# Six-stage transformer kernel: new order for the first two cell blocks, maxima through TensorE, ffn weight preparation inside the scan stage

## The reference, cut to what matters

```python
x = x + _L0_xattn_ref(_layernorm(x), ctx_1024, ctx_1024, mask, ...)   # masked cross attention, 16 heads
x = x + _L0_attn_ref(_layernorm(x), context, Wq, Wk, Wv, Wout, bout)  # wide attention, 8 heads of 128, over 2 x 512 context rows
x = x + _L0_ffn_ref(_layernorm(x), ew, act_w, We, be, Wq, ...)        # cell: 6 nodes, each an attention over earlier nodes, edge weights We
x = x + _L1_xattn_ref(_layernorm(x), ctx_1024)                        # plain attention on the context
x = x + _L1_attn_ref(_layernorm(x), A, W_b, ..., W_o, b_o)            # scan: h[t] = a[t] h[t-1] + u[t], 16 states per sequence
x = x + _L1_ffn_ref(_layernorm(x), W_fc, ..., B_proj)                 # ffn 256 -> 1024 -> 256

# in the ffn, for W_fc and W_proj alike:
scale = jnp.max(jnp.abs(w)) / 127
wq = jnp.clip(jnp.round(w / scale), -128, 127) * scale
Wq = w + (wq - w)
y = x @ Wq.T + b + 2.0 * ((x @ A.T) @ B.T)                            # rank 16
```

## Time and profile before

| | |
|---|---|
| median of 3 runs | 3278.88 us (3271.15 to 3282.62) |
| the profiled execution | 3276.0 us, span 3274.2 us, mean TensorE clock 0.963 of full |
| PE busy | 3023.0 us (92%) |
| DVE / ACT / POOL busy | 2199.9 / 2009.3 / 926.0 us |
| stages by the first work of each, us from the span's start | wide 658, cell 1678, ctx about 2050, scan 2914.6, ffn 3029.4 |

### The profile page before, as it was taken

One profiled execution on the slowest core, in us unless ns is written; L12 is line 12 of the kernel. 1 busy time (PEld: TensorE's weight loads), 2 busy tenths in 40 slices (PEclk: granted clock), 3 DMA queues, 4 the chain that ended last, 5 costly groups with the idle time before them and its releaser, 6 DMA issues. The chain is left out here.

```text
span 3274.2 us, 88570 instructions
## 1 busy us (share of the span) xinstructions
PE 3023.0 (92%) x34175; PEld 2461.8 (75%) x34175; DVE 2199.9 (67%) x5201; ACT 2009.3 (61%) x3697; POOL 926.0 (28%) x800
## 2 busy tenths in 40 slices
PE   8999999959999999999977999999999997878699
PEld 6888888737877877877866887787787786544598
DVE  5777777756666666666634778778778776664643
ACT  5777777647767667767733666666666675332353
POOL 3444444336555555655620000000000000110110
PEclk9999999969999999999988999999999999889699
DMA  2112111148887888887973111111111110741200
GB/s 79 58 59 66 62 58 58 38 104 151 150 136 145 150 136 148 152 146 140 173 197 119 34 41 53 47 41 47 54 41 47 47 34 24 230 141 52 88 20 26
DMA packets 664877, 294.34 MB, mean 90 GB/s; under 512 B 550747, under 2 KB 639792, under 8 KB 664576
## 3 DMA queue, kind: packets, MB, share of 16 engines
q1 hardware_dynamic: 626176, 237.71, 34.1%
q10 hardware_dynamic: 38400, 52.44, 4.8%
HBM read 125.95 MB, written 29.88 MB: 48 GB/s over the span
## 5 line engine op out<-in xcount | busy, mean ns | idle before, releaser
L1096 POOL TENSOR_TENSOR wide_parts<-wide_prob,wide_parts 128x1024 f16<-128x1024 f32 x256 | 548.7, 2143 | 398.1 <-ACT wide_parts L1282 329.9
L1385 DVE TENSOR_REDUCE wide_row_max<-wide_score 128x1 f32<-128x1024 f32 x256 | 312.7, 1221 | 163.2 <-PE wide_score L1130 161.6
L1130 PE MATMUL wide_score<-wide_kT,wide_qT 128*128 128x512 f32 x1536 | 413.1, 404 | 7.1 <-ACT wide_prob L1270 5.5
L1270 ACT ACTIVATE wide_prob<-wide_score,wide_neg_max 128x1024 f32<-128x1024 f32 x256 | 285.2, 1114 | 163.7 <-DVE wide_neg_max L1388 158.2
L641 ACT ACTIVATE mask_prob<-mask_prob,mask_row_min 128x256 f32<-128x256 f32 x512 | 232.1, 503 | 161.6 <-DVE mask_row_min L730 161.6
L1130 PEld LDWEIGHTS wide_score<-wide_kT,wide_qT 128*128 128x128 f32 x1536 | 277.1, 189 | 67.9 <-issue 8.9
L1282 ACT ACTIVATE wide_parts<-wide_prob 128x1024 f16<-128x1024 f32 x256 | 269.9, 1054 | 18.5 <-ACT wide_prob L1270 9.2
L2217 DVE TENSOR_REDUCE cell_row_max<-cell_score 128x8 f32<-128x512 f32 x192 | 131.2, 684 | 171.6 <-PE cell_score L1853 169.8
L1146 PE MATMUL wide_turn<-wide_probT,wide_v 128*128 128x256 f16 x1536 | 189.6, 273 | 2.8 <-DMA wide_probT<-wide_parts 2.8
L1146 PE MATMUL wide_pv<-wide_probT,wide_v 128*128 128x256 f16 x1536 | 190.3, 274 | 1.2 <-DMA wide_probT<-wide_parts 1.2
L111 POOL TENSOR_TENSOR cell_var_eps<-cell_mean_var,const_eps 128x4 f32<-128x4 f32 x8 | 1.6, 200 | 670.5 <-DVE cell_mean_var L105 670.5
(11 more groups left out here) (338 smaller groups left out, 6878.3 us busy)
## 6 DMA issues: line engine op xcount, KB each, us to landing
cell_w_stage<-cell_weights ACTq DMA_DIRECT2D x24, 768.0 KB, 6.0
mask_ctx<-in_ctx SPq DMA_DIRECT2D x32, 512.0 KB, 3.9
ctx_ctx<-in_ctx SPq DMA_DIRECT2D x32, 512.0 KB, 4.4
mask_mask<-in_mask_BxS_ik SPq DMA_DIRECT2D x32, 256.0 KB, 4.0
wide_probT<-wide_parts SPq DMA_TRANSPOSE x512, 3.3
cell_w_stage<-in_L_ffn_We ACTq DMA_DIRECT2D x24, 256.0 KB, 2.7
cell_w_stage<-in_L_ffn_Wo ACTq DMA_DIRECT2D x24, 256.0 KB, 3.1
mask_x_ln<-in_x SPq DMA_DIRECT2D x32, 128.0 KB, 2.1
```

The lines of the kernel that those rows point to most:

```text
L1096: pool.tensor_tensor(parts[:, s % 2, LO, :], prob[:, s % 2, :], parts[:, s % 2, HI, :], ALU.subtract).then_inc(part_lo, 1)
L1130: mm = pe.matmul(score[:, s % 2, half * 512:(half + 1) * 512], qT[:, u_par, a, s * P:(s + 1) * P], kT[:, par, b, half * 512:(half + 1) * 5 ...
L1270: act.activation(prob[:, s % 2, :], score[:, s % 2, :], ACT.Exp, bias=neg_max[:, s % 2:s % 2 + 1], scale=SHARP, accum_out=row_sum[:, u_par ...
L1385: dve.tensor_reduce(row_max[:, one], score[:, s % 2, :], AX.X, ALU.max).then_inc(max_found, 1)
```

## The change

It does four things.

1. Wide: the two maxima are shared over the partitions by PE and DVE. PE transposes the 128x2 tile of maxima into 2x128, DVE reduces it to 2x1 and writes it out as a 2x128 row, PE transposes that back to 128x2 (in `misc_ps`). POOL has no reduce any more. W_v's load is issued ahead of block 1's x, and POOL adds all its biases after all eight `rstd_of`.
2. Cell: block 1 is turned into the two `acc` banks right behind block 0's projections and ahead of block 0's scores, and its projections go in the order q, k, v as the `score` banks come free. The edge and output weights of node 0 are loaded by ACT during the making of the fused weights, and split ahead of everything of block 1.
3. Scan and ffn: the tiles of the ffn's weights and x stay in one memory over both stages (`FfnWeights`). The weights are loaded at the end of scan's loads, and their preparation is cut into pieces that stand in scan's steps 1 to 7. It uses three banks (3, 6, 7) and no `partition_all_reduce`; POOL takes the rest of the split weights (`gpsimd_lo`). Scan's steps are all written out.
4. x stays in SBUF between scan and ffn: no store of it, no load. ffn's first `fc` waits for all of both weights (`w_lo`), and at the very end one more clear of semaphores with its barrier stands.

Where the preparation's pieces stand in scan, and what ffn begins with:

```diff
@@ scan, POOL
-        with pool.Fori(0, NBLK) as n:
+        for n in range(8):
             norm.gpsimd_rstd(pool, n)
+        ffn.gpsimd_lo(pool, 0, ffn.loras)
@@ scan, PE
         def project_out(n, j, first):
             pe.wait_ge(state_done, n + 1)
+            if n == 7:
+                ffn.tensor_turn(pe, ffn_banks, ffn.fc_turns, len(ffn.turns))
...
         def step(n, j, first):
             project_out(n, j, first)
+            if n == 3:
+                ffn.tensor_share_max(pe, ffn_banks[2])
             if follows(n, 2):
                 norm.tensor_turn(pe, n + 2, True)
                 project_in(n + 2, j, False)
+            if n == 2:
+                ffn.tensor_max_rows(pe, ffn_banks[2])
+            if n == 4:
+                pe.wait_ge(ffn.quant_step, 1)
+                ffn.tensor_turn(pe, ffn_banks, 0, ffn.small_turns)
+            if n == 5:
+                ffn.tensor_turn(pe, ffn_banks, ffn.small_turns, ffn.fc_turns)
+            if n == 6:
+                ffn.tensor_low_rank(pe, ffn_banks, 0, ffn.fc_loras)
...
         steps(pe, step)
+        ffn.tensor_low_rank(pe, ffn_banks, ffn.fc_loras, ffn.loras)
@@ scan, ACT: behind copy and gate of block n+2
-            store(n)
+            if n == 4:
+                ffn.scalar_copy(act, ffn_banks, 0, ffn.small_turns)
+            if n == 5:
+                ffn.scalar_copy(act, ffn_banks, ffn.small_turns, ffn.fc_turns)
+            if n == 6:
+                ffn.scalar_hi(act, 0, ffn.fc_loras)
+            if n == 7:
+                ffn.scalar_copy(act, ffn_banks, ffn.fc_turns, len(ffn.turns))
+                ffn.scalar_hi(act, ffn.fc_loras, ffn.loras)
@@ scan, DVE
             if follows(n, 1):
                 scan(n + 1, 1 - j)
+            if n in (1, 2):
+                ffn.vector_max(dve, n - 1)
+            if n == 3:
+                ffn.vector_spread_max(dve, ffn_banks[2])
+            if n == 4:
+                ffn.vector_quantise(dve, ffn_banks[2], 0)
+            if n == 5:
+                ffn.vector_straight_through(dve, 0)
+            if n == 6:
+                ffn.vector_straight_through(dve, 1)
             finish(n)
+            if n == 5:
+                ffn.vector_quantise(dve, ffn_banks[2], 1)
+            if n == 6:
+                ffn.vector_merge(dve, ffn_banks, 0, ffn.fc_loras)
+            if n == 7:
+                ffn.vector_merge(dve, ffn_banks, ffn.fc_loras, ffn.loras)
@@ the three banks of the preparation: each use waits for the copy or merge of the use three before
+        i = self.uses.index((kind, n))
+        if i >= 3:
+            before, m = self.uses[i - 3]
+            pe.wait_ge(self.prep_copied if before == "turn" else self.weights_ready, m + 1)
+        return banks[i % 3]
@@ ffn, DVE
-        find_max(0)
...
+        normalise(0)
+        normalise(1)
         turned_lo(0)
-        weights(0, FC_LORAS)
-        normalise(1)
-        quantise(1)
         pairs(dve, step)
@@ ffn, POOL
-        share_max(0)
         norm.gpsimd_rstd(pool, 0)
-        share_max(1)
-        pool.wait_ge(small_loaded, SMALL_LOADED)
         add_bias(0)
```

The cell's part:

```diff
@@ cell, PE
-        for X in range(2):
-            scores_free(X)
-            turn_input(X, X)
-            if X == 0:
-                pe.wait_ge(set_lo, 2)
-            pe.wait_ge(proj_copied, X * 6 + DH)
-            project_v(0, X)
-            project_k(0, X)
-            project_q(X * DH, 0, 0, X)
-            scores(X * DH, (X + 1) * 6)
+        turn_input(0, 0)
+        pe.wait_ge(set_lo, 2)
+        pe.wait_ge(proj_copied, DH)
+        project_v(0, 0)
+        project_k(0, 0)
+        project_q(0, 0, 0, 0)
+        turn_input(1, 1, acc)
+        scores(0, 6)
+        pe.wait_ge(proj_copied, 6 + DH)
+        project_q(DH, 0, 0, 1)
+        scores_free(1, DH)
+        project_k(0, 1)
+        scores_free(1)
+        project_v(0, 1)
+        scores(DH, 2 * 6)
@@ cell, ACT
             if n == 4:
+                load_own(0)
                 act.wait_ge(staged, 1)
...
+        copy_input(0, 0)
+        split_own(1, 0)
...
+        copy_input(6, 1, acc)
+        act.wait_ge(stage_stored[0], STORED)
+        act.dma_start(w_stage[:, FUSED_AT:SET], set_dram[0]).then_inc(set_loaded, 16)
+        copy_q(DH, 0, 0)
+        for r in range(ROW):
+            exp(0, r, 0)
+        copy_k(6 + DH, 0)
+        copy_v(6 + 2 * DH, 1)
...
         copy_early(2 * DH)
-        split_own(1, 0)
+        act.wait_ge(set_loaded, 48)
         split_fused(1)
@@ cell, DVE
         input_rest(0, 0)
         normalise(1, 1, None)
+        split_own(1, 0)
+        input_rest(1, 1, acc)
         subtract_max(0, 0, range(ROW))
...
-        input_rest(1, 1)
-        split_own(1, 0)
@@ wide, POOL
-        for n in range(2):
-            rstd_of(n)
-        for m in range(2):
-            pool.wait_ge(top_found, m + 1)
-            pool.partition_all_reduce(all_top[:, m:m + 1], top[:, m:m + 1], P, RMAX).then_inc(top_shared, 1)
-        for n in range(2, NBLK - 1):
+        for n in range(NBLK):
             rstd_of(n)
```

453 lines of the change are left out of this document (226 added, 227 removed).

## The result

The kernel after takes 3225.69 us in the median of four runs (3221.27 to 3228.62), the kernel before on the same chip 3275.92 (3271.15 to 3282.62): a ratio of 0.9844, with a 95% interval from 0.9822 to 0.9867, or 44 to 58 us less. I had said 3238, 38 us less than the profiled execution. The profiled execution of the kernel after took 3225.7 us, 50.3 less than that of before.

The account below looks back on a forecast made before the run. PE, busy for 92% of the span, was taken as the bound, with gains where it stands still: 3276.0 - 8.5 - 14.4 + 1.6 - 17.5 + 1.0 = 3238.2 us, given as 3238; range 3225 to 3253.

Parts of the forecast that it names:

- wide's opening: Start of wide: the wait on POOL's reduces goes, so block 2's copy comes earlier; 8.5 us gained, bounds 6.9 and 10.
- cell's opening: Cell up to the first `add_edge`: the new order removes PE's waits; 14.4 us gained, bounds 11 and 15.5.
- delays in scan up to `project_out(7)`, with 0.9 for slower turns: Scan before its last `project_out`: inserted preparation adds 0.4, then 2.1, 2.7 and 7.0 us in steps 4, 5, 6; turns 0.9.
- from there to the first `fc`: Start of `project_out(7)` to ffn's first `fc`: 11.5 us less, although `project_out(7)` runs at the low clock.
- first block of ffn: First to second `fc` in ffn: 25.9 us for 43.4 without W_proj's preparation between; 17.5 us gained.
- barrier at the end: End of the kernel: the further barrier costs 1.0 us, between 0 and 1.5.
- The products of step 6 bring the clock down: Scan, step 6: the rank-16 products make PE's granted clock fall from 2.4 to 1.2 GHz.
- `project_out(7)` then takes 12.6 instead of 6.8, as it did in step 0: Scan's last `project_out`: it runs at the low clock throughout, taking 12.6 us instead of 6.8.
- the clock stays up: Rival, scan's last steps: full clock is kept, -5.6 us instead of +1.6 up to the first `fc`; 3231 us, chance 0.24.
- the upper bound of the forecast: Wide: at most 10 us gained, all of POOL's shift.
- The 0.4 that I had taken off for the fused weights behind it: Cell, behind the first `add_edge`: the remaining fused weights come some 0.4 us later in relation, so 14.4 for 14.8.

## Why the prediction was right or wrong

The sum's terms against the two profiles, in us:

| term | forecast | measured |
|---|---|---|
| wide's opening | -8.5 | -11.6 |
| cell's opening | -14.4 | -14.7 |
| delays in scan up to `project_out(7)`, with 0.9 for slower turns | +13.1 | +12.2 |
| from there to the first `fc` | -11.5 | -18.6 |
| first block of ffn | -17.5 | -17.6 |
| barrier at the end | +1.0 | -0.1 |
| mask, wide's scores, cell's preparation and the rest | 0 | +0.1 |

**The step that failed** is the length of the low clock. "The products of step 6 bring the clock down" was right, and the run with 128 rows shows why: it is their few rows. "`project_out(7)` then takes 12.6 instead of 6.8, as it did in step 0" was wrong: it took 7.5 (3003.46 to 3010.97). I had taken step 0 as the pattern for how long the clock stays low, and had not asked what PE does in between. In step 0 PE goes from its pause straight into `project_out`, a third of whose products have 17 rows. In step 6 sixteen turns of full rows stand between. The run with these turns moved away gave 12.7 us, the forecast's number, and the run with the state on 128 rows left 3 of the 20 us of low clock in steps 0 and 1. Whether any other 3.7 us of full-row work would do as the turns did was not tried. Of the 7.1 us by which this stretch came out shorter than forecast, `project_out(7)` makes 5.1; 1.2 are in the products and subtractions behind it (7.5 for 8.7), 0.3 in the barrier and 0.6 from block 0's statistics to the first `fc` (11.0 for 11.6). The other 5 us that the forecast fell short by are mostly wide's (3.1), the barrier's at the end (1.1) and scan's delays' (0.9). The rival "the clock stays up" had nearly this number (-5.6 for scan's delays and the handover together, measured -6.4) by a mechanism that did not happen.

**Wide** was right in kind and 1.5 us too small: the reduces cost 10.0, the upper bound of the forecast. The term took 8.5 of a shift of 8.9 for block 2's copy (699.81 to 690.9); in the run with the old orders and no reduce, where the clock rose as late as before, this copy stands at 690.10. The other 1.6 of the 11.6 come from the clock's earlier rise, which the change did not make.

**Cell** was right in its waits: the ones that go, and ACT's copies of v as what is late next. That 29.6 us were forecast for 29.7 is in part luck: up to the early turn it was 0.7 us faster than I had worked out, and the early turn, at the low clock, 0.8 slower (1.97 us for 1.09 before). The 0.4 that I had taken off for the fused weights behind it can't be told in rows that vary by 10.

**Scan's delays** in steps 4, 5 and 6 came out as 1.9, 2.4 and 7.8 for 2.1, 2.7 and 7.9 (7.0 and the 0.9 of the turns), and those before as 0.1 for 0.4: the waits behind ACT's copies hold PE at the ends of steps 4 and 5. DVE held `project_out` nowhere.

**ffn's first block** took 25.8 us (3030.45 to 3056.25) for 25.9 forecast. The barrier cost nothing that the profiles show.

The last row of the table is a sum of shifts that the change did not make: -0.6 in mask, -1.2 in wide's scores, +2.5 in cell's preparation, -0.6 behind it. Such shifts are as large in runs of one and the same code, so a tenth of a us in a term is luck as far as the total goes.

## What to carry to other kernels

Ask of every stretch of TensorE work how many rows its operands have, not only how long PE is busy: a few products with few rows among full ones cost here 0.4 us at each pair of changes, and kept a clock that was low at 1.2 GHz while PE was busy without a gap (at the full clock the same mix did not bring it down, in steps 2 to 5); products with few rows back to back brought it down. Filling them up with zeros cost no time in any run here. When a low clock is carried over from one place of a profile to another, compare the instructions between, not the busy share. And a wait without a name on POOL, ahead of and behind a partition reduce, goes with the reduce (in scan only the one ahead of it could be seen); it is free where nobody waits for POOL.
